# Issue order of small indirect DMAs and turn points in a fused graph-attention front stage

## The reference, cut to what matters

```python
x = layernorm(x)
z = einsum('ni,hoi->nho', x, Wfc)              # 3750 x 512 by 512 x 512
s_src = einsum('nho,ho->nh', z, a_src)         # one score per node and head
s_dst = einsum('nho,ho->nh', z, a_dst)
e = leaky_relu(s_src[src] + s_dst[dst])        # 60000 edges x 8 heads
m = segment_max(e, dst); ex = exp(e - m[dst])
alpha = ex / segment_sum(ex, dst)[dst]
```

## Time and profile before

| | us |
|---|---|
| median of three runs | 3844.43 (3841.66, 3844.43, 3853.0) |
| profiled execution, its own time | 3842.01 |
| its span | 3839.9 |
| pick loop of layer 0 / layer 1 | 215 to 465 / 2292 to 2526 |
| busy: PE, DVE, ACT, POOL | 2893.6, 2186.5, 571.9, 1612.2 |
| score gathers on POOL (line 378) | 320, 985 ns mean |
| scatters on POOL (line 397) | 60, 1139 ns mean |
| granted TensorE clock, mean | 0.874 of full |

### The profile page before, as it was taken

One profiled execution on the slowest core, in us unless ns is written; L12 is line 12 of the kernel. 1 busy time (PEld: TensorE's weight loads), 2 busy tenths in 40 slices (PEclk: granted clock), 3 DMA queues, 4 the chain that ended last, 5 costly groups with the idle time before them and its releaser, 6 DMA issues. The chain is left out here.

```text
span 3839.9 us, 37939 instructions
## 1 busy us (share of the span) xinstructions
PE 2893.6 (75%) x9194; PEld 1392.2 (36%) x9195; DVE 2186.5 (57%) x3514; ACT 571.9 (15%) x968; POOL 1612.2 (42%) x1595
## 2 busy tenths in 40 slices
PE   5977718999886881499995897835899987539990
PEld 2433312233222551355552343412222222436660
DVE  5776686666653876533221413487666664974444
ACT  2100110000002650011110210011000000411210
POOL 0666107777760000144441166404777774002216
PEclk9988859999998875699998898967999998559995
DMA  4325207777761221156554436304777774143337
GB/s 154 86 92 91 104 11 210 210 211 211 211 196 48 83 75 57 30 142 154 140 143 124 106 87 135 102 14 120 211 210 211 211 210 125 61 154 120 120 112 244
DMA packets 330788, 512.22 MB, mean 133 GB/s; under 512 B 172499, under 2 KB 178115, under 8 KB 329999
## 3 DMA queue, kind: packets, MB, share of 16 engines
q0 software_dynamic: 113824, 311.79, 30.0%
q1 hardware_dynamic: 92975, 194.62, 14.4%
q10 hardware_dynamic: 123840, 3.94, 1.8%
HBM read 423.29 MB, written 86.92 MB: 133 GB/s over the span
## 5 line engine op out<-in xcount | busy, mean ns | idle before, releaser
L1015 PE MATMUL bank<-aggregate_zg,aggregate_onehot 128*128 x2112 | 1092.0, 637 | 162.8 <-issue 120.6
L953 POOL DMA_INDIRECT aggregate_zg<-z_rows,src_groups x940 | 888.7, 945 | 660.0 <-POOLq L2211 335.5
L994 DVE TENSOR_TENSOR aggregate_zg<-aggregate_zg,bank 128x1024 f32<-128x1024 f32 x470 | 573.5, 1220 | 470.4 <-DMA aggregate_zg<-z_rows,src_groups 470.2
L1015 PEld LDWEIGHTS bank<-aggregate_zg,aggregate_onehot 128*128 128x128 f32 x2112 | 351.6, 192 | 901.9 <-issue 895.2
L378 POOL DMA_INDIRECT front_d<-src_scores,src_chunks x320 | 315.1, 985 | 266.6 <-DMA front_d<-src_scores,src_chunks 92.1
L1623 POOL DMA_INDIRECT exp_xg<-hn_rows,exp_gather_tok x64 | 72.0, 1124 | 531.9 <-DVE exp_gather_tok L1685 411.3
L676 PE MATMUL bank<-front_w,front_table 128*120 128x512 bf16 x960 | 246.2, 394 | 20.1 <-DVE front_w L553 20.1
L1767 PE MATMUL bank<-exp_w,exp_h_t 128*117 128x512 f32 x512 | 225.7, 595 | 0.7 <-ACT exp_h_t L1714 0.7
L974 DVE TENSOR_TENSOR aggregate_onehot<-bank,columns 128x256 f32<-128x256 f32 x528 | 215.0, 416 | 0.0
L939 ACT COPY acc<-bank 128x512 f32<-128x512 f32 x60 | 35.1, 585 | 1193.6 <-PE bank L1015 1193.6
L1759 PE MATMUL bank<-exp_xg_t,exp_w 128*128 128x468 f32 x512 | 206.1, 561 | 0.7 <-ACT exp_xg_t L1703 0.7
(11 more groups left out here) (390 smaller groups left out, 3565.6 us busy)
## 6 DMA issues: line engine op xcount, KB each, us to landing
exp_w<-in_L_ffn_w SPq DMA_DIRECT2D x32, 1024.0 KB, 7.8
slot_out<-exp_y SPq DMA_DIRECT2D x66, 256.0 KB, 2.0
z_rows<-front_z SPq DMA_DIRECT2D x60, 256.0 KB, 2.0
hn_rows<-fin_xn SPq DMA_DIRECT2D x20, 768.0 KB, 3.5
aggregate_zg<-z_rows,src_groups POOLq DMA_INDIRECT x940, 3.7
front_early<-src_key SPq DMA_DIRECT2D x16, 640.0 KB, 4.0
front_early<-src_tile SPq DMA_DIRECT2D x16, 640.0 KB, 4.2
front_edge<-src_key SPq DMA_DIRECT2D x16, 640.0 KB, 4.0
```

Source lines behind the costliest of these rows:

```text
L953: pool.indirect_dma_start(zg[:, r, j, :], None, k.z_rows[:, :], bass.IndirectOffsetOnAxis(k.src_groups[:, n:n + 1], 0)).then_inc(gathered[ ...
L994: v.tensor_tensor(z, z, bcast_last(scales[:, at:at + J * H], DH), ALU.mult).then_inc(msg_ready, 1)
L1015: mm = nc.tensor.matmul(k.banks[:, bass.ds(bank, 1), :].rearrange("p a n -> p (a n)"), onehot[:, n % RING, j, :], zg[:, bass.ds(at, 1), j, ...
```

## The change

Three edits. The two kinds of wait inside GpSimd's gathers and scatters are removed, in both layers. In layer 0's table of turns the first 14 d blocks move from picks 22 + 3n to 28 + 3n, and the last two gathered blocks from picks 38 and 54 to 45 and 65. Layer 1's table stays, and so do the waits of PE and ACT for whole blocks and for all scatters.

```diff
--- before.py
+++ after.py
@@ -41,7 +41,7 @@
 DR = 5
 PICKS = CH * TBLK
 PICKS_BEFORE = (3, 0)
-TURNS_AT = ({**{22 + 3 * n: ("d", n) for n in range(GC - 1)}, 72: ("d", GC - 1), **{m: ("g", i) for i, m in enumerate((4, 9, 14, 38, 54))}},
+TURNS_AT = ({**{28 + 3 * n: ("d", n) for n in range(GC - 1)}, 72: ("d", GC - 1), **{m: ("g", i) for i, m in enumerate((4, 9, 14, 45, 65))}},
             {**{4 + 4 * n: ("d", n) for n in range(GC - 1)}, 78: ("d", GC - 1), **{m: ("g", i) for i, m in enumerate((2, 7, 21, 37, 53))}})
 OH = 4
 HT = NT // 2
@@ -373,8 +373,6 @@
                         for c in range(CH):
                             n = (i * J + j) * CH + c
                             at = (i * J + j) * P + c * H
-                            if c % 8 == 4:
-                                pool.wait_ge(gathered[i * J + j], 16 * c)
                             pool.indirect_dma_start(picked[:, at:at + H], None, k.src_scores[:, :],
                                                     bass.IndirectOffsetOnAxis(k.src_chunks[:, n:n + 1], 0)).then_inc(gathered[i * J + j], 16)
 
@@ -392,8 +390,6 @@
                     pool.wait_ge(first_ready, 1)
                     pool.wait_ge(table_filled, 16)
                 for n in range(NT):
-                    if n % 8 == 4:
-                        pool.wait_ge(scattered, 16 * n)
                     pool.indirect_dma_start(k.first_scores[:, :], bass.IndirectOffsetOnAxis(k.first_edge[:, n:n + 1], 0),
                                             s_dst_nodes[:, n, :], None).then_inc(scattered, 16)
                 if layer == 1:
```

## The result

The changed kernel takes 3757.89 us (median of 4 runs, 3753.46 to 3761.99) where the kernel before, measured beside it, takes 3843.05 us (4 runs, 3839.38 to 3853.0). The ratio is 0.9773, with a 95% interval of 0.9754 to 0.9791. The profiled execution took 3758.3 us (span 3756.2) against 3842.0 before, 83.7 us less; forecast were 85 less.

A forecast was written before the change was run, and what follows sets the result against it. The prediction took POOL's pausing stream of score gathers and scatters, for which PE waits, to bound both pick loops. 3842.0 - 42 (layer 0) - 43 (layer 1) = 3757 us, range 3747 to 3780.

The forecast's parts named there:

- POOL's pace: Score gathers and scatters in both layers: without pauses 1.25 us per gather and 1.26 per scatter, against 1.48 before.
- (a): Rival: landings set the pace, so layer 1 keeps its time and layer 0 gains 24: 3818 us; chance 0.11 with higher POOL means.
- (c): Rival: descriptor writing slows, up to 1.87 us per op, making the kernel slower from 1.61 on: 3941 us; chance 0.03.
- (b): Rival: POOL's layer 1 mean exceeds 1.25, each 0.05 us costing 9.5 us; forecast including it up to 1.33: chance 0.84.
- Layer 0: Layer 0's pick loop: a gain of 42 us, from 20.5 + 17.1 + 4.4.
- the waits of 26.1, 1.6 and 17.1: PE's waits in layer 0 for the first d block, for ACT behind it, and at two gathered blocks: all go.
- the new stall at pick 23: Layer 0: DVE's 8.16 us scan, formerly covered by PE's long wait, now stalls PE for 7.2 us.
- slow stretches behind waits: Layer 0: PE's slow running behind the two gathered-block waits goes too, 2.2 us each, 4.4 in all.
- Layer 1: Layer 1's pick loop: last gathered block turned 41.7 us earlier, plus a slow stretch of 1.5: a gain of 43 us.
- PE and POOL meet: Layer 1: PE and POOL reach the last gathered block within a microsecond of each other, and it is turned at about 2423.
- the gain of 20.5: Layer 0's first d turn, moved from pick 22 to 28: waits of 26.1 and 1.6 go, a 7.2 us stall comes.
- The rule weighed: Shared ports of DVE and POOL: DVE behind POOL counted as free; by the skill's rule at most 1 us per long DVE op.

The follow-up runs named there:

- e5: Changed kernel with layer 0's two DVE boundary scans replaced by copies of the same size; 3741.13 us, ratio 0.972 to the kernel before.
- e6: Changed kernel with DVE's wide boundary steps in layer 0 cut into pieces, spread over the picks; 3736.97 us, ratio 0.972 to the kernel before.
- e4: Changed kernel with the waits inside the scatters put back, in both layers; 3763.82 us, ratio 0.979 to the kernel before.
- after: The changed kernel itself, all three edits against the kernel before; 3757.89 us, ratio 0.9773.
- e1: Changed kernel with the old table of turns back, so only the pauses are removed; 3762.01 us, ratio 0.977 to the kernel before.
- e2: Kernel before with only the new table of turns, pauses kept; 3824.26 us, ratio 0.994 to the kernel before.
- e10: Changed kernel with e6's pieces and layer 1's first turns behind ACT's ten loads, on the second chip; 4457.54 us, ratio 1.059 to the kernel before.
- e12: e10 with POOL's pauses in gathers and scatters put back, on a third chip; 4113.06 us, ratio 0.983 to the kernel before.
- e9: Changed kernel with layer 1's first turns behind ACT's ten loads, on the second chip; 4474.64 us, ratio 1.064 to the kernel before.
- e11: e7 with SP's boundary load in layer 1 put behind the key rows of block 13, second chip; 4475.19 us, ratio 1.064 to the kernel before.
- e8: Changed kernel with e6's pieces in layer 0 and e7's later turns in layer 1; 3734.18 us, ratio 0.972 to the kernel before.
- e7: Changed kernel with later turns in layer 1, d blocks from pick 11; 3756.9 us, ratio 0.977 to the kernel before.

## Why the prediction was right, and what it did not see

**POOL's pace: right.** 1.268 us per op against 1.26 in the sum, the old pauses gone, the ops at 0.95 us except beside DVE. Rivals (a) and (c) are refuted on this chip, and (b) stays at the lower end: the mean is 1.27 in layer 1.

**Layer 0: right, 42.6 against 42.** The last scatter at 261.17, the waits of 26.1, 1.6 and 17.1 gone, and the new stall at pick 23 of 7.33 against 7.2. PE's waits fell from 61.2 to 23.7 us, 37.5 in all; the other 5.1 are slow stretches behind waits, for which the sum had 4.4. e5 and e6 show that this stall was named rightly: with the scans cut up, it goes. e4 shows that POOL has slack in this layer.

**Layer 1: right, 42.7 against 43.** From the first scatter to the turn of the last gathered block are 2381.39 - 2138.07 = 243.3 us; the forecast had 2423 - 2180.25 = 242.8. That PE and POOL meet there is shown by three runs: no wait in `after`, 3.23 in e1, 3.41 in e4. That the gain came within half a microsecond is in part luck: the same code gave loops of 188.8 to 191.3 us.

**The step that the sum didn't separate.** It told of the turns' move as if the gain of 20.5 needed it ("the first d turn moves from pick 22 to pick 28"). e1 shows that the removal of the pauses brings all of it alone, within a microsecond. The moved turns matter only while the pauses are there (16.1 us of layer 0 in e2's trace, 24.4 us of the whole by the medians), and 42.6 is not the sum of its parts.

**Rival (a)'s price.** It gave 24 us to the turns alone, with the last block at 405.1 "as before". By the medians of e2 that came out (24.4); by its trace it did not, since in the traced execution the block was turned at 417.25: there POOL's ops met DVE's scans in full, and more ops took 1.3 to 1.9 us. The forecast counted the scans for the changed kernel, and took the old arrival for the rival. Which of the two is the typical case was not settled by a second trace.

**The rule weighed.** POOL was held behind DVE again (4.34, 4.84, 8.64, 8.75 us), and DVE was not held behind POOL: its op at 219.97 took 4.15 us although POOL's scatter before the held one was at work until 220.3. The sum without that cost stands.

**What no rival had.** The slower case of the prediction, (c), was descriptor writing that gets slower, from a mean of 1.61 us. On the second chip POOL's ops kept their 0.95 us and their 1.25 us pace; what got slow, while the stream ran, was PE (a start each 2.8 us) and the hand-over from PE to ACT and DVE. The prediction took the pauses for pure loss; e10 and e12 say that on such a chip they act as a throttle. `after` itself didn't run there, but e9 and e11 have its layer 0 unchanged, and by those 100 us it would be slower than before. Why PE starts its matmuls so late is open, and so is whether the number of small indirect transfers in flight decides it: nothing here changes that number in steps, and the same stream leaves PE alone on the first chip.

**The way past both kernels.** On the first chip e6 and e8 beat both (3737 and 3734 us). The pieces don't depend on the missing pauses: e12, with pieces and pauses, is 1.7% faster than before on a slow chip. e12 wasn't run on the first chip, and how its 71 us there divide among pieces, turns and order of loads wasn't tried.

## What to carry to other kernels

When an in-order queue feeds several consumers, work out the arrival of its last item from the bare issue pace and compare it with the time at which the consumer gets there; the gain ends where the two meet, and the next long op of another engine is what is then seen. Cut such an op into pieces that fit between two steps, even at the same total. And before a wait in a stream of small indirect transfers is removed because "it only pauses", ask what else moves in that stretch and try it on more than one chip. Here the same edit is worth -2.3% on one, and costs about +6% in kernels that contain it on another.

## What was not expected of the hardware

- Chips differ: the kernel before took 3841 to 3849, 4206 and 4184 us on three of them, and on the slow ones the 470 gathers of an aggregation took 762 and 764 us, not 605, while a packet took 0.18 us on all three.
- On the second chip, while POOL issued one small indirect DMA each 1.25 us, PE started the matmuls of a chain without semaphores 2.8 us apart, where 16 of them had taken 0.55 us; a 256 KB store issued in the midst of it had moved within 5 us.
- A count of packets says how much was asked for as well as how much got through: 864 plain packets in place of 4176 came from late tiles, and not from a full queue.
- ACT's issue of the same ten loads took 13.6, 15.9, 16.7, 19.5 and 31.6 us in different places. The two longest, 31.6 and 31.8 in e7 and e8, are the only ones with SP's load of the boundaries beside them; in e9, e11 and e12, where that load comes later, they took 21.5, 21.0 and 20.8. That points to the load, but on the first chip the order of e7 was not run without it.
